# One program region from the neighbourhood attention to the soft experts, and one activation table for logarithm and exponential

## The chip, the cores and the metric

The kernel runs on one core of a Trainium2 chip, in float32 with a few bfloat16 matrix products. The metric is the device time of one launch in microseconds. A core has five engines that each run their own instruction queue in order: TensorE (PE, matrix products; the weight loads are listed apart as PEld), VectorE (DVE), ScalarE (ACT), GpSimd (POOL) and SyncE (SP, which issues most DMAs). They meet only through semaphores: an instruction waits until a counter has a value, and another engine's instruction raises it.

## The reference

Input are 32 rows of 512 token ids; the width is D = 64. With LN for a layer norm without parameters:

```
h = token_features(x)
h = h + neighbourhood_attention(LN(h))     # 8 heads, 31 neighbours, dilation 2
h = h + mixture(LN(h))                     # 8 experts, top 2 by a router, exact gelu
h = h + decayed_attention(LN(h))           # (q k^T / 8) * 0.99^(i-j), i >= j, no softmax
h = h + soft_experts(LN(h))

soft_experts(x):  feat = mean(x, batch);  w = softmax(feat @ Wr + br)        # [512, 8]
  a = relu(bn1(x @ W1[e] + b1));  a = relu(bn2(a @ W2[e] + b2))
  out = sum over e of (a @ Wo[e] + bo) * w[:, e]
```

## The kernel before

Two batch rows share a tile, 64 channels of each on 128 partitions by 512 tokens, so there are NP = 16 such pairs. `s.h` holds the running sum and `s.z` the normalised input of a stage. Every stage is a software pipeline written out by hand: `unrolled(count, unroll, (lead, step), ...)` emits each engine's steps in one fixed order, and `wait_ge` and `then_inc` tie the engines together. `done(n)` is n + 17, because the engine that frees a buffer first gives 16 credits (`give_credits`); a consumer that comes before the credits waits for them.

An `nc.Block()` is one program region. At its end all five engines meet at a barrier. Before the change there are six of them: preparation, token features, neighbourhood attention with the mixture of experts (these two already share one), `decayed_attention`, `soft_router` and `soft_experts`. The text calls the three joins between the last four stages seam A (mixture to decayed attention), seam B (decayed attention to soft router) and seam C (soft router to soft experts).

The layer norm has a side chain: POOL squares the pair (`square`, L488), PE sums the squares over channels (`variance`, L495), ACT turns them into a reciprocal deviation by Ln and Exp, SP sends the result through DRAM and back to all partitions (`hop`, `spread`, tiles `n_bc`), and POOL multiplies (`scaled`, L535). Four pairs go together. The last four pairs of a stage are scaled without DRAM, by PE (`near`, L2086) and DVE (L2155). In the mixture Ln and Exp run on ACT between gelu calls, twice: `last_deviations` (L1600, L1602) and `deviations` for n = 1 (L1642, L1644).

`soft_router` is a chain with little to overlap: the last four normalised pairs, PE sums of all 16 (`sums_of`, L2090), copy, logits, softmax on DVE and ACT, turn (L2112), copy (L2134), spread to expert weights (L2118), copies into `f1_w` (L2137, L2171) and `f1_r` (L2173). Then `soft_experts` runs 64 steps of `first` (PE L2225), `relu` (ACT L2272), `second` (PE L2235), `weigh` (DVE L2292), `third` (PE L2247), and per pair a residual (DVE L2303, L2306). `first` and `relu` need no router weights; `second` and `weigh` do. `keep_warm` (L502) issues small products whose results nobody reads.

## Time and profile before

| | us |
|---|---|
| median of 3 runs | 862.85 (859.15 to 865.65) |
| the profiled execution, its device time | 860.88 |
| its span from the first to the last instruction | 859.2 |
| PE busy in the span | 797.3 (93%) |
| DVE, ACT, POOL busy | 582.8, 480.8, 301.9 |

The span is the time between the first and the last recorded instruction; 1.7 us of the execution lie around it. Busy matrix products are pipelined records, so 93% does not say that PE works at its peak, only that it has little empty time. Idle time of an engine matters where the others wait for it.

### The profile page before, as it was taken

What the parts mean: (1) busy time and instruction counts of PE and PEld (TensorE: products, weight loads), DVE (VectorE), ACT (ScalarE), POOL (GpSimd) and SP (SyncE); (2) the same over time, 40 slices, a digit from 0 to 9 for tenths busy, and PEclk for the clock granted to TensorE, in tenths of its full rate; (3) what the DMA queues carried; (4) which work ended last, traced back from release to release, by engine and by line L of the source; (5) the groups of instructions that cost most, each with busy time, mean ns of one, the idle gap of its engine ahead of it and who ended that gap; (6) DMA issues with size and microseconds to landing.
All of it is one profiled execution on the core that took longest, in us unless ns stands there. A gap on an engine that the chain in (4) does not pass through costs nothing. (4 is left out here: it accounts for less than half of the span.)

```text
span 859.2 us, 28916 instructions
## 1 busy us (share of the span) xinstructions
PE 797.3 (93%) x12645; PEld 407.8 (47%) x12645; DVE 582.8 (68%) x853; ACT 480.8 (56%) x660; POOL 301.9 (35%) x292
## 2 busy tenths in 40 slices
PE   3989799999999999799899899899998899999996
PEld 2222377776676676523333233476663233333332
DVE  5537477777776776678687956577772477777776
ACT  2244477787777777666666766322222455555553
POOL 3225463543553442113453455465452900000000
PEclk9999899999999999999999999999999999999998
DMA  4210221001002001000200310153321011111111
GB/s 107 30 32 1 87 65 41 4 4 65 4 5 65 5 4 65 3 2 1 62 2 1 99 50 2 26 174 100 98 76 37 14 50 50 50 44 40 43 51 37
DMA packets 38670, 36.38 MB, mean 42 GB/s; under 512 B 20817, under 2 KB 25074, under 8 KB 38418
## 3 DMA queue, kind: packets, MB, share of 16 engines
q1 hardware_dynamic: 37474, 32.52, 13.5%
q8 instruction: 101, 1.65, 0.8%
q10 hardware_dynamic: 1072, 2.02, 0.7%
q14 instruction: 23, 0.19, 0.1%
HBM read 18.79 MB, written 7.34 MB: 30 GB/s over the span
## 5 line engine op out<-in xcount | busy, mean ns | idle before, releaser
L2272 ACT ACTIVATE se_a<-se_p,cols 128x512 f32<-128x512 f32 x128 | 92.8, 775 | 75.9 <-PE se_p L2225 75.9
L2292 DVE SCALAR_TENSOR_TENSOR se_a<-se_p,cols,z 128x1024 f32<-128x1024 f32 x64 | 82.2, 1284 | 48.9 <-PE se_p L2235 48.9
L1264 DVE TENSOR_REDUCE na_rowmax<-na_ps 128x16 f32<-128x1024 f32 x64 | 78.1, 1220 | 53.5 <-PE na_ps L1108 53.5
L1589 ACT ACTIVATE z<-me_p,cols 128x512 f32<-128x512 f32 x128 | 81.1, 685 | 53.9 <-PE me_p L1511 51.2
L1772 DVE TENSOR_TENSOR me_gw<-me_pc,z 128x1024 f32<-128x1024 f32 x64 | 78.3, 1223 | 45.1 <-PE me_pc L1528 36.8
L944 POOL TENSOR_TENSOR z<-na_k,const 128x512 f32<-128x512 f32 x62 | 63.0, 1047 | 127.8 <-ACT na_k L1186 127.8
L488 POOL TENSOR_TENSOR n_sq<-h 128x512 f32<-128x512 f32 x64 | 68.5, 1075 | 82.5 <-DVE h L858 39.8
L1546 PE MATMUL me_py<-me_gw,w_out 64*64 64x512 f32 x512 | 90.9, 607 | 0.0
L1511 PE MATMUL me_p<-z,moe_w 64*64 64x512 f32 x512 | 82.3, 611 | 2.0 <-ACT z L1589 2.0
L535 POOL TENSOR_TENSOR z<-h,n_bc 128x512 f32<-128x512 f32 x58 | 74.4, 1297 | 23.8 <-DMA n_bc<-n_spread 23.8
L1267 DVE TENSOR_TENSOR z<-na_ps,na_rowmax 128x1024 f32<-128x1024 f32 x64 | 78.4, 1225 | 2.2
L1117 PE MATMUL na_pt<-const,z 128*128 128x128 f32 x512 | 70.1, 280 | 5.3 <-ACT z L1213 3.1
L1213 ACT ACTIVATE z<-z 128x1024 f32<-128x1024 f32 x64 | 67.4, 1053 | 7.1 <-DVE z L1267 6.4
L2225 PE MATMUL se_p<-z,f_w 64*64 64x512 f32 x512 | 68.7, 603 | 2.0 <-ACTq L548 1.1
L2235 PE MATMUL se_p<-se_a,f_w 64*64 64x512 f32 x512 | 68.2, 598 | 1.3 <-DVE se_a L2292 1.3
L1220 ACT ACTIVATE na_et<-na_pt 128x1024 f32<-128x1024 f32 x64 | 65.4, 1021 | 6.7 <-PE na_pt L1117 5.9
L2247 PE MATMUL se_py<-se_a,w_out 64*64 64x512 f32 x512 | 67.4, 589 | 0.5 <-DVE se_a L2292 0.5
L1117 PEld LDWEIGHTS na_pt<-const,z 128*128 128x128 f32 x512 | 56.8, 142 | 21.0 <-issue 15.1
L1108 PE MATMUL na_ps<-z,na_q 32*32 32x256 f32 x2048 | 51.2, 386 | 0.6 <-issue 0.5
L1131 PEld LDWEIGHTS na_po<-na_v,na_et 128*32 128x32 f32 x4096 | 41.6, 110 | 21.1 <-ACT na_et L1220 11.4
L1207 ACT ACTIVATE na_v<-na_pm 64x512 f32<-64x512 f32 x64 | 38.6, 603 | 21.4 <-PE na_pm L1063 21.0
L1131 PE MATMUL na_po<-na_v,na_et 128*32 128x18 f32 x4096 | 48.0, 187 | 1.6 <-issue 0.9
(363 smaller groups left out, 1260.9 us busy)
## 6 DMA issues: line engine op xcount, KB each, us to landing
n_bc<-n_spread SPq DMA_DIRECT2D x116, 128.0 KB, 3.1
z<-z SPq DMA_DIRECT2D x64, 128.0 KB, 2.4
out<-se_rows SPq DMA_DIRECT2D x16, 256.0 KB, 2.1
n_spread<-n_rstd SPq DMA_DIRECT2D x12, 256.0 KB, 2.0
const<-in_const ACTq DMA_DIRECT2D x1, 1114.0 KB, 7.4
const<-in_const ACTq DMA_DIRECT2D x1, 562.0 KB, 4.5
f_w<-in_L_ffn_W SPq DMA_DIRECT2D x4, 128.0 KB
const<-in_const ACTq DMA_DIRECT2D x1, 258.0 KB, 2.9
```

Of the source, the lines that this page charges most:

```text
L535: return eng.tensor_tensor(row(s.z, p), row(s.h, p), s.bc[p % 4][:], ALU.mult)
L1117: mm = nc.tensor.transpose(p_t[:, c, :], e[b][:, 2 * c:2 * c + 2, :].rearrange("p h w -> p (h w)"), const(s, "ident"))
L1131: mm = nc.tensor.matmul(p_o[QT * t:QT * t + QT, at_col:at_col + 18], et[b][:, head, QT * t:QT * t + QT], v[j % 2][:, par * 4 + t, b, head, ...
L1264: nc.vector.tensor_reduce(rowmax[b][:], scored, AX, ALU.max).then_inc(s_max, 1)
L1267: nc.vector.tensor_tensor(e[b], scored, rowmax[b][:].unsqueeze(2).broadcast_to([128, GROUPS, WIN]), ALU.subtract).then_inc(s_diff, 1)
L1511: mm = nc.tensor.matmul(hidden(at.n, b)[half[e2], :], s.moe_w1[half[b], 2 * ep + e2, :], row(s.z, at.of(4))[half[b], :], start=True, stop= ...
L1546: mm = nc.tensor.matmul(p_y[half[b], e2, :], s.moe_w2[half[e2], ep, :], gw[at.k % 2][half[e2], b, :], start=(ep == 0 and b != e2), stop=(e ...
L1589: nc.scalar.activation(g[at.n % 7][:, b, :], hidden(at.n, b)[:], ACT.Gelu, bias=col(s, "moe_b1", ep)).then_inc(s_g, 1)
L1772: nc.vector.tensor_tensor(gw[at.k % 2][:], p_c[:], g[at.n % 7], ALU.mult).then_inc(s_gw, 1)
L2225: mm = nc.tensor.matmul(hidden(at.n, e2)[half[b], :], s.f1_w1[half[e2], 2 * ep + e2, :], z[half[e2], :], start=True, stop=True, skip_group ...
L2272: nc.scalar.activation(a1[at.k % 2][:, e2, :], hidden(at.n, e2)[:], ACT.Relu, scale=col(s, "f1_g1", 2 * ep + e2), bias=col(s, "f1_be1", 2 ...
L2292: nc.vector.scalar_tensor_tensor(out=a2[at.k % 2][:], in0=p_2[:], scalar=col(s, "f1_be2", ep), in1=s.f1_w[:, ep, :].unsqueeze(1).broadcast ...
```

## The change

The last three blocks are gone: `decayed_attention`, `soft_router` and `soft_experts` put their instructions behind those of the mixture in the same region, and their semaphores live as long as it does. Where the barriers kept order, single waits do now: POOL clears the attention's state once the mixture's last sum is done (`s_end`), PE's first `scores` wait for the mixture's sums to leave their PSUM banks, SP waits for `s_qk`, and `second` and `weigh` wait for the router's copies (`s_taken`, `s_kept`).

Work is moved over the seams too. The last `variance`, Ln and Exp of the attention are issued in the router's code, PE having eight `sums_of`, the scale product and the shift product ahead of them. Pairs 9 to 11 are scaled by DVE in place of POOL. The four `near` products signal one by one. `first(0)` and `first(1)` stand around the expansion of the weights on PE, `relu(0)` between the router's copies on ACT. POOL's 16 additions of `f1_r` are paced by `first`. Five groups of `keep_warm` go or shrink: 7 to 0, 8 to 0, 8 to 3, 4 to 2, 8 to 0; one of 2 is new.

The mixture loads the table set with both logarithm and exponential ahead of each Ln, where a set was loaded for Ln and another for Exp. The attention loads it behind its second `fetch`, the router not at all.

```diff
-                if at.n == EP * NP - 1:
-                    keep_warm(nc, s, p_r[:], 7)
...
+                    sc.preload_act_table_set("natural_log_exp_and_others")
...
+                        nc.vector.tensor_tensor(row(s.h, i), row(s.h, i), odd[slot][:], ALU.add).then_inc(s_end, 1)
...
-        block = ctx.enter_context(nc.Block())
...
+            pool.wait_ge(s_end, 1)
...
-                if p >= 6:
+                if 6 <= p < NP - 1:
...
-            normal(NP - 6)
-            normal(NP - 5)
...
+                if at.n == 0:
+                    te.wait_ge(s_even, done(NP - 1))
+                    te.wait_ge(s_odd, done(NP - 1))
...
-            spreads(NP // 4 - 1, NP - 1)
-            keep_warm(nc, s, p_s[:, 0, :], 8)
...
-            sc.preload_act_table_set("natural_log_exp_and_others")
             give_credits(sc, s_qkd)
 
             def former(at):
                 if at.n > 0:
                     return
+                sc.preload_act_table_set("natural_log_exp_and_others")
...
-            deviations(NP // 4 - 1)
...
-        p_sums, p_scale, p_small, p_shift, *p_wide = [ps(x) for x in ("psums", "pscale", "psmall", "pshift", "pwide0", "pwide1", "pwide2", "pwide3")]
...
+        *p_near, p_sums, p_small, p_shift, p_scale, p_last = [ps(x) for x in ("pnear0", "pnear1", "pnear2", "psums", "psmall", "pshift", "pscale", "plast")]
+        p_near.append(p_last)
+        p_wide = [p_small, p_shift, p_scale, p_last]
...
+                sp.wait_ge(s_qk, done(NP - 2 + p))
...
-            for j in range(4):
-                mm = nc.tensor.matmul(p_wide[j][:], const(s, "near")[group(j), :], s.rstd[group(j), LAST, :], start=True, stop=True, skip_group_check=True)
-            mm.then_inc(s_near, 1)
...
-            for p in range(ENDS[0]):
+            for p in range(8):
...
-            te.wait_ge(s_z, 4)
+            te.wait_ge(s.n_z, nth(3, 8))
+            sums_of(8)
+            te.wait_ge(s.n_sq, nth(3, NP - 1))
+            variance(nc, s, LAST, p_small).then_inc(s.n_var, 1)
+            te.wait_ge(s.n_z, nth(3, 11))
+            for p in range(9, 12):
+                sums_of(p)
+            keep_warm(nc, s, p_near[0][:], 2)
+            te.wait_ge(s.n_rstd, quad(3, LAST))
+            for j in range(4):
+                nc.tensor.matmul(p_near[j][:], const(s, "near")[group(j), :], s.rstd[group(j), LAST, :], start=True, stop=True,
+                                 skip_group_check=True).then_inc(s_near, 1)
             for p in ENDS:
+                te.wait_ge(s_z, p - ENDS[0] + 1)
                 mm = sums_of(p)
             mm.then_inc(s_sums, 1)
             keep_warm(nc, s, p_small[:], 3)
...
-            keep_warm(nc, s, p_shift[:], 8)
+            keep_warm(nc, s, p_near[2][:], 3)
+
+        def expand_weights(te):
             te.wait_ge(s_copies, 1)
...
-            keep_warm(nc, s, p_small[:], 4)
+            keep_warm(nc, s, p_small[:], 2)
...
-            keep_warm(nc, s, p_small[:], 8)
+            nc.tensor.matmul(p_sums[:], shift[:], by_expert[0:32, :], start=True, stop=True, skip_group_check=True).then_inc(s_shifted, 1)
...
-            sc.preload_act_table_set("natural_log_exp_and_others")
...
+            sc.wait_ge(s.n_var, quad(3, LAST))
+            nc.scalar.activation(s.rstd[:, LAST, :], p_small[:], ACT.Ln, bias=s.eps[:]).then_inc(s.n_ln, 1)
+            sc.wait_ge(s.n_ln, 8 + LAST)
+            nc.scalar.activation(s.rstd[:, LAST, :], s.rstd[:, LAST, :], ACT.Exp, scale=-0.5).then_inc(s.n_rstd, 1)
...
+
+        def fetch_turned_weights(sc):
             sc.wait_ge(s_turned, 1)
...
+        def fetch_weights(sc):
             sc.wait_ge(s_wide, 1)
             for ep in (0, 2):
-                nc.scalar.activation(s.f1_w[:, ep, :], p_wide[ep][:], ACT.Copy)
+                nc.scalar.activation(s.f1_w[:, ep, :], p_wide[ep][:], ACT.Copy).then_inc(s_taken, 1)
...
-            ve.wait_ge(s_near, 1)
-            for p in ENDS:
-                v.tensor_tensor(row(s.z, p), p_wide[p % 4][:], row(s.h, p), ALU.mult).then_inc(s_z, 1)
+            ve.wait_ge(s.n_z, nth(3, 8))
+            for p in range(9, 12):
+                ve.wait_ge(s.n_bc[p % 4], spread_done(3, p))
+                scaled(nc.vector, s, p).then_inc(s.n_z, 1)
             ve.wait_ge(s_scale, 1)
             w2 = s.f1_w2[:].rearrange("p a b -> p (a b)")
             v.scalar_tensor_tensor(out=w2, in0=p_scale[:], scalar=float(HID), in1=w2, op0=ALU.mult, op1=ALU.mult)
+            for p in ENDS:
+                ve.wait_ge(s_near, p - ENDS[0] + 1)
+                v.tensor_tensor(row(s.z, p), p_near[p % 4][:], row(s.h, p), ALU.mult).then_inc(s_z, 1)
...
-                v.tensor_copy(s.f1_w[:, ep, :], p_wide[ep][:])
...
-            v.tensor_copy(s.f1_r, p_shift[:])
...
+            v.tensor_copy(s.f1_r, p_sums[:]).then_inc(s_kept, 1)
...
+            pool.wait_ge(s_kept, 3)
             for p in range(NP):
+                if p >= 2:
+                    pool.wait_ge(s_w1, done(EP * (p - 1)))
...
+                if at.n == 0:
+                    te.wait_ge(s_taken, 2)
+                    te.wait_ge(s_kept, 3)
...
-            unrolled(EP * NP, 8, (3, first), (2, second), (1, third), (0, turn))
+            def next_first(at):
+                if at.n >= 2:
+                    first(at)
+
+            first(Step(0, 0, 8))
+            expand_weights(te)
+            first(Step(0, 1, 8))
+            unrolled(EP * NP, 8, (3, next_first), (2, second), (1, third), (0, turn))
...
-            unrolled(EP * NP, 8, (0, fetch_odd), (3, relu))
+            def next_relu(at):
+                if at.n >= 1:
+                    relu(at)
+
+            fetch_turned_weights(sc)
+            relu(Step(0, 0, 8))
+            fetch_weights(sc)
+            unrolled(EP * NP, 8, (0, fetch_odd), (3, next_relu))
...
+                if at.n == 0:
+                    ve.wait_ge(s_taken, 2)
+                    ve.wait_ge(s_kept, 2)
...
+            sums = mixture_of_experts(nc, s, r, inner, block)
+            s_qk = decayed_attention(nc, s, inner, block, *sums)
+            weights = soft_router(nc, s, inner, block, s_qk)
+            soft_experts(nc, s, out, inner, block, *weights)
```

ACT in the mixture, from the router's copy to the return to gelu. The names are tiles: `n_rstd` the deviations, `me_odd` half of the expert sum, `me_pr` a PSUM bank. Before:

```order
L1577 ACTIVATE me_logits_t<-me_pr 128x512 [waits me_rt,me_rl]
L1600 ACT_TABLE_LOAD
L1600 ACTIVATE n_rstd<-n_rstd,eps 128x512 [waits me_last]
L1602 ACT_TABLE_LOAD
L1602 ACTIVATE n_rstd<-n_rstd 128x512 [waits n_s_ln]
L1610 ACTIVATE me_odd<-me_py 128x512 [waits me_hz,me_w2]
L1589 ACT_TABLE_LOAD [waits me_gw]
```

And changed:

```order
L1576 ACTIVATE me_logits_t<-me_pr 128x512 [waits me_rt,me_rl]
L1599 ACT_TABLE_LOAD [waits me_last]
L1600 ACTIVATE n_rstd<-n_rstd,eps 128x512
L1602 ACTIVATE n_rstd<-n_rstd 128x512 [waits n_s_ln]
L1610 ACTIVATE me_odd<-me_py 128x512 [waits me_hz,me_w2]
L1588 ACT_TABLE_LOAD [waits me_gw]
```

One table load stands there in place of two; the same holds at L1642 to L1644.

PE at seam B, from the attention's last variance to the sums of pairs 12 to 15. Before:

```order
L495 MATMUL da_pw<-n_sq,const 32x512 [waits n_s_sq,da_st]
L495 MATMUL da_pw<-n_sq,const 32x512 x3
L502 MATMUL da_ps<-pick_b,ident_b 128x512 x8
L1802 UNCONDITIONAL_BRANCH
L2083 UNCONDITIONAL_BRANCH [waits barrier_Pool_Activation_PE_DVE_SP_release]
L2086 MATMUL sr_pwide<-n_rstd,const 128x512 x4
L2090 MATMUL sr_psums<-z,w_in 32x512 x12
L2094 MATMUL sr_pscale<-bn_diag,const 128x512
L2097 MATMUL sr_pshift<-f_wdup,const 32x128 x4
L2090 MATMUL sr_psums<-z,w_in 32x512 [waits sr_z]
```

And changed, starting right behind the attention's last output product:

```order
L2090 MATMUL sr_psums<-z,w_in 32x512 x8
L2094 MATMUL sr_pscale<-bn_diag,const 128x512
L2097 MATMUL sr_pshift<-f_wdup,const 32x128 x4
L2090 MATMUL sr_psums<-z,w_in 32x512 [waits n_s_z]
L495 MATMUL sr_psmall<-n_sq,const 32x512 [waits n_s_sq]
L495 MATMUL sr_psmall<-n_sq,const 32x512 x3
L2090 MATMUL sr_psums<-z,w_in 32x512 [waits n_s_z]
L2090 MATMUL sr_psums<-z,w_in 32x512 x2
L502 MATMUL sr_pnear<-pick_b,ident_b 128x512 x2
L2110 MATMUL sr_pnear<-n_rstd,const 128x512 [waits n_s_rstd]
L2110 MATMUL sr_pnear<-n_rstd,const 128x512 x2
L2110 MATMUL sr_plast<-n_rstd,const 128x512
```

The independent sums, the scale and the shift moved from behind the `near` products to ahead of the variance; the sums of pairs 12 to 15 (`[waits sr_z]`) now follow `near` directly.

PE at seam C, from the turn of the weights on. Before:

```order
L2118 MATMUL sr_pwide<-sr_by_expert,const 128x512 [waits sr_by_expert]
L2118 MATMUL sr_pwide<-sr_by_expert,const 128x512 x3
L2121 MATMUL sr_pshift<-sr_by_expert,sr_shift 128x512 [waits sr_shift]
L502 MATMUL sr_psmall<-pick_b,ident_b 128x512 x8
L2051 UNCONDITIONAL_BRANCH
L2213 UNCONDITIONAL_BRANCH [waits barrier_Pool_Activation_PE_DVE_SP_release]
L2225 MATMUL se_p<-z,f_w 64x512 [waits se_s_a1,n_s_swapped0]
L2225 MATMUL se_p<-z,f_w 64x512 x3
L2225 MATMUL se_p<-z,f_w 64x512 [waits se_s_a1]
```

And changed:

```order
L2253 MATMUL se_p<-z,f_w 64x512 [waits se_s_a1,n_s_swapped0]
L2253 MATMUL se_p<-z,f_w 64x512 x3
L2126 MATMUL sr_psums<-const,sr_copies 128x128 [waits sr_copies]
L2126 MATMUL sr_psums<-const,sr_copies 128x128 x3
L502 MATMUL sr_psmall<-pick_b,ident_b 128x512 x2
L2132 MATMUL sr_psmall<-sr_by_expert,const 128x512 [waits sr_by_expert]
L2132 MATMUL sr_pshift<-sr_by_expert,const 128x512
L2132 MATMUL sr_pscale<-sr_by_expert,const 128x512
L2132 MATMUL sr_plast<-sr_by_expert,const 128x512
L2135 MATMUL sr_psums<-sr_by_expert,sr_shift 128x512 [waits sr_shift]
L2253 MATMUL se_p<-z,f_w 64x512 [waits se_s_a1]
```

`first(0)` (L2225, now L2253) moved ahead of the turn and `first(1)` directly behind the shift product.

## Rows read from the trace of the kernel before

**Rows 1.** Windows: PE, PEld, DVE, ACT, POOL busy; PE clock, DMA share, GB/s.

```profile
416.00:418.00 2.00, 2.00 (x16) 0.67 (x12) 0.00 (x0) 0.00 (x0) 0.00 (x0) 0.51 0.35 118
...
720.00:740.00 20.00, 20.00 (x184) 7.38 (x180) 14.80 (x23) 11.00 (x16) 0.00 (x0) 1.00 0.15 42
```

**Rows 2.** Timeline at the first Ln and Exp of the mixture.

```profile
411.57 1.28 ACT L1602 ACT_TABLE_LOAD   x1
...
413.40 0.58 ACT L1610 ACTIVATE me_odd<-me_py 128x512 f32<-128x512 f32 x1
414.08 0.69 PE L1542 MATMUL me_py<-me_ct,w_out 64*64 64x512 f32 x2 [3.09 <-issue]
418.62 1.27 ACT L1589 ACTIVATE z<-me_p,cols 128x512 f32<-128x512 f32 x2 [3.34 <-PE me_p L1511]
```

**Rows 3.** Timeline at the second Ln and Exp of the mixture.

```profile
478.60 1.28 ACT L1644 ACT_TABLE_LOAD   x1
...
483.98 1.09 PE L1511 MATMUL me_p<-z,moe_w 64*64 64x512 f32 x8 [1.22 <-ACT z L1589]
```

**Rows 4.** Timeline where neighbourhood attention meets the mixture, without a barrier.

```profile
365.95 0.66 PE L1511 MATMUL me_p<-z,moe_w 64*64 64x512 f32 x4
```

**Rows 5.** Timeline at seam A.

```profile
543.18 0.60 ACT L1610 ACTIVATE me_odd<-me_py 128x512 f32<-128x512 f32 x1 [3.37 <-PE me_py L1546]
...
543.91 0.69 DVE L1784 TENSOR_TENSOR h<-h,me_odd 128x512 f32<-128x512 f32 x1
...
544.99 1.28 ACT L1971 ACT_TABLE_LOAD   x1 [1.21 <-PEq L2363]
...
546.42 1.09 PE L1909 MATMUL da_pqk<-z,w_in 64*64 64x512 f32 x8 [1.69 <-ACT L1971]
```

**Rows 6.** Timeline at seam B, to the copy of the sums.

```profile
644.13 0.94 PE L1947 MATMUL da_py<-da_qd,da_state 128*128 128x128 f32 x6 [0.24 <-DVE da_state L2036]
...
645.87 1.04 POOL L488 TENSOR_TENSOR n_sq<-h 128x512 f32<-128x512 f32 x1 [1.36 <-DVE h L2042]
...
647.06 1.94 PE L495 MATMUL da_pw<-n_sq,const 128*32 128x512 f32 x8 [1.99 <-POOL n_sq L488]
...
649.05 0.69 ACT L1994 ACTIVATE n_rstd<-da_pw,eps 128x512 f32<-128x512 f32 x1 [10.32 <-PE da_pw L495]
...
649.77 0.63 ACT L1996 ACTIVATE n_rstd<-n_rstd 128x512 f32<-128x512 f32 x1
...
651.67 1.14 PE L2086 MATMUL sr_pwide<-n_rstd,const 32*128 32x512 f32 x8 [0.30 <-PEq L1802]
...
652.74 2.78 PE L2090 MATMUL sr_psums<-z,w_in 128*32 128x512 f32 x24
652.87 2.48 DVE L2155 TENSOR_TENSOR z<-sr_pwide,h 128x512 f32<-128x512 f32 x4 [7.08 <-PE sr_pwide L2086]
...
656.51 0.95 PE L2097 MATMUL sr_pshift<-f_wdup,const 128*32 128x128 f32 x7
...
658.52 0.60 ACT L2130 ACTIVATE sr_sums<-sr_psums 128x512 f32<-128x512 f32 x1 [0.64 <-PE sr_psums L2090]
```

**Rows 7.** Timeline from the router's turned weights over seam C.

```profile
662.91 0.60 ACT L2134 ACTIVATE sr_by_expert<-sr_psums 128x512 f32<-128x512 f32 x1 [1.74 <-PE sr_psums L2112]
...
664.87 1.08 ACT L2137 ACTIVATE z<-sr_pwide 128x512 f32<-128x512 f32 x2 [1.37 <-PE sr_pwide L2118]
...
666.08 0.68 DVE L2173 COPY z<-sr_pshift 128x512 f32<-128x512 f32 x1
...
668.55 1.09 PE L2225 MATMUL se_p<-z,f_w 64*64 64x512 f32 x8 [1.08 <-ACTq L548]
669.70 1.45 ACT L2272 ACTIVATE se_a<-se_p,cols 128x512 f32<-128x512 f32 x2 [3.75 <-PE se_p L2225]
...
674.24 1.28 DVE L2292 SCALAR_TENSOR_TENSOR se_a<-se_p,cols,z 128x1024 f32<-128x1024 f32 x1 [7.48 <-PE se_p L2235]
```

**Rows 8.** Timeline of DVE at the first residual of the soft experts.

```profile
686.47 1.56 DVE L2306 TENSOR_TENSOR se_res<-se_res,se_odd 128x512 f32<-128x512 f32 x1
```

36 lines of the change are left out of this document (17 added, 19 removed).

## The prediction

> **What bounds the kernel now.** I read the windows of 20 us first, to see whether an engine sets the pace, and then the timeline at the places that the change touches, following at each the wait that ends last.
>
> In the soft experts PE is busy without a gap at full clock: 20.00 of 20 us, clock 1.00 [rows 1]. Nothing in the change makes those 64 steps shorter, so time can only come from the places where PE stands still. There are five.
>
> In the mixture ACT interrupts its gelu for Ln and Exp. At the first place PE sits idle for 3.09 us until 414.08 [rows 2]; what ends it is the copy `me_odd`, which ACT finishes at 413.98 behind two table loads. PE's granted clock then falls to the lower level of 1.2 GHz, 0.51 over 416 to 418 [rows 1], and the next gelu starts only at 418.62. At the second place PE waits 1.22 us for ACT [rows 3].
>
> At seam A the last copy of the mixture ends at 543.78, but the attention's first product starts at 546.42: it waits for ACT, whose table load from 544.99 to 546.27 stands ahead of the credits that PE needs [rows 5]. At seam B PE's last output product ends at 645.07, the squares come at 646.91, the variance takes 1.94 us instead of the 1.09 that eight such records take elsewhere (the clock has dropped in the gap), Ln and Exp end at 650.40, the barrier costs until 651.67, and then PE does twelve sums, scale and shift although the pairs that the chain waits for were ready at 655.35; the copy of the sums starts at 658.52 [rows 6, 7]. At seam C the last copy of the router ends at 666.76, and DVE's first `weigh` starts at 674.24, since `first`, `relu`, `first`, `second` fill the pipeline only then [rows 7].
>
> **Do joints without a barrier cost anything?** The kernel already has one, between neighbourhood attention and mixture: PE's first product there starts at 365.95 with no idle time in its row [rows 4]. I take zero for the branch that remains.
>
> **The tables.** At the first place one load of 1.28 us goes [rows 2]. ACT reaches `me_odd` 1.28 earlier, and that copy is what PE waits for: 1.3 us. Bounds: 0 if another wait is right behind it; and up to 1.3 + 2.3 if the shorter idle time (3.09 - 1.28 = 1.81) also keeps the clock up, as half of the 4.54 us from 414.08 to 418.62 is what the lower clock can cost at most. Idle times of 1.69 at seam A left the clock alone, judging by the 1.09 of the eight records behind it [rows 5], and 1.99 at seam B did not [rows 6]; 1.81 lies between, so I count only the 1.3. At the second place the load saved is also 1.28, the wait that it can shorten is 1.22 [rows 3]: 1.2, bounds 0 and 1.28. Sum 2.5.
>
> From the start of the load at 411.57 to the copy at 413.40 pass 1.83 us, and an Exp lies between them [rows 2]: there is room for the 1.28 of the load and for little else. The Trainium skill, page "ScalarE: Activation LUTs", section "What ACT_TABLE_LOAD costs", gives about 1283 ns for the load and 1380 ns of drain on top, 2.66 us for a switch. By that price the two places would give 2.8 us more on ACT. The rows agree on the 1283 and leave no room for the drain, so the sum goes by the rows.
>
> **Seam A.** The table load moves behind the second `fetch`, where ACT waits for the next variance anyway; nobody waits for it there, and if that cover were too short it would cost at most its 1.28. The credits for the first product now stand right behind `me_odd`, which ends at 543.78 [rows 5]. So the product starts at about 543.9 instead of 546.42: 2.5 us. The values on DVE wait for POOL's clearing of the state, which now waits for the sum that ends at 544.60 [rows 5]; with a short clearing that is about 545.2, and the value products, behind the 1.09 us of the first, are done at about 546.1. The added wait is hidden by 0.9 us; everything queued behind it on POOL is the last square, which nobody needs yet. PE's new wait ahead of the first scores is for sums that are out of PSUM by 543.91, when DVE goes on to the next [rows 5], long before the scores' own inputs. The removed seven `keep_warm` leave PE idle for 0.8 us, less than the 1.69 that did no harm. Bounds 1.3 (ACT's load still in the way) and 3.3 (start at the end of the mixture's last product). Take 2.5.
>
> **Seam B.** PE after 645.07 does, without a barrier: eight sums at 2.78/12 = 0.23, 1.85; the scale, 655.52 to 656.51, 1.0; the shift, 0.95; one more sum, 0.23. That is 649.1 [rows 6]. POOL's squares are ready at 646.91, so the variance, which waits for nothing else, starts 2.0 us later than before. At full clock it takes 1.09 and ends at 650.2, 1.2 later than before. Ln and Exp 0.69 and 0.63: 651.6. The first `near` signals alone, 1.14/4 = 0.3: 651.95. DVE's four products take 2.48: 654.4. PE has nothing else left, so the last sum ends at about 654.75 and the copy starts at 654.8 against 658.52: 3.7 us. On the way DVE does three scalings of 0.69 (an addition of the same shape, [rows 5]) from 645.8, which must be done when PE comes to their sums at 650.2: 2.1 us of work in 4.4 us. Their data come from eight DMAs that landed before POOL used them. If POOL's square is held up by them, it has 2.0 us of slack. Bounds: 2.0 (the clock drops again while PE idles between the four products, and the small products behind take twice their time) and 4.5 (sums hidden better than I count). Take 3.7.
>
> That slack matters, because DVE and POOL do get in each other's way here: the residual with both inputs in SBUF took 1.56 us while POOL was adding [rows 8], and an addition of the same shape took 0.69 with POOL free [rows 5]. The Trainium skill, page "SBUF — State Buffer", section "SBUF: two separate sides", calls the shared pair an exclusive lock that whoever starts first keeps for the whole instruction. It speaks against putting the scalings on DVE just when POOL squares; by it the square could start up to 0.69 later, which the 2.0 us absorb, so the sum is the same.
>
> **Seam C.** The chain from the copy of the sums (658.52) to the end of `by_expert` (662.91 + 0.60) keeps its 5.0 us, except that `first(0)` stands before the turn on PE. It waits for ACT's credits, which stand behind the router's Exp, and then takes 1.09; DVE's four softmax steps run meanwhile. Bounds 0 and 1.09; I take 0.3. In the old times plus 0.3: `relu(0)`, 1.45, ends at 665.3, ACT's two copies, 1.08, at 666.4, DVE's `f1_r` at 667.06 [rows 7]. `second(0)` starts there, takes 1.09, and `weigh(0)` starts at 668.25 instead of 674.24: 6.0 us. `first(1)` and `relu(1)` are done by 668.1 and are not late, and with PE busy the drop of the clock that the pipeline's start had before has no gap to come from. SP's new waits for `s_qk` end with the attention's last projections, before the seam, with nothing but the fetches for the experts queued behind them. The eight `keep_warm` that go here cost nothing, because `first(1)` stands in their place. Bounds: 4.5 and 7.
>
> POOL's additions are spread out and leave the first residual alone: at most 0.87 [rows 8, 5], a part of which PE hides. Take 0.2.
>
> **Sum.** 2.5 + 2.5 + 3.7 + 6.0 + 0.2 = 14.9 us. The profiled execution took 860.9 (1.7 us around its span), so it becomes 846.0. The median of the three runs is 862.85, 2.0 above the profiled one, with runs from 859.15 to 865.65; against it the forecast is **848.0 us**, 1.7% faster. About 1% (8.6 us) is what a measurement of this kernel can tell from no change.
>
> **Rivals.**
>
> *The clock falls once more, and part is given back* (chance 0.15). 28 `keep_warm` products go on balance, and in seam B PE does only 0.23 us of work for each 0.62 us of DVE. If the clock drops there, what PE does until the experts run (logits, turn, spread, `first`, `second`: about 5 us at full clock on the chain) takes up to twice as long. For: the 1.94 us of the variance [rows 6] show that such a gap is enough. Against: ahead of it PE now has 5 us of unbroken work. Price 3 to 5: 851 to 853.
>
> *The clock stays up in the mixture* (0.17). The idle time of 1.81 is short enough, and the timing at the second place improves likewise. 2 to 4 us more: 844 to 846.
>
> *It does not do what it says* (0.07). The seams are serial chains, and only the waits for the barrier go, about 1.2 us of them at each seam by ACT's idle 1.21 [rows 5]; with the tables 3.6 + 2.5 = 6: about 857. Against: rows 6 and 7 show the work that is overlapped, and the queues of the changed kernel show it moved.
>
> *Slower: POOL's additions collide in every pair* (0.03). Before, the 16 additions of about 1.27 us ran in one go and could meet one residual or two. Now one runs per pair, 16 in all, and a collision of DVE's two-input residual with one costs 0.87 [rows 8, 5], at most the 1.27 of the whole addition. DVE's delay reaches PE over the residual, its turn and the PSUM bank. It decides from 14.9/16 = 0.93 us per pair; at 1.27 the kernel would take 868. Against: the addition for pair p is released by `first` of the pair before, two pipeline steps (5 us) ahead of the residual.
>
> The forecast itself has 0.58, its own range being 845 to 851. The range for 8 in 10 takes in both clock cases and the runs' scatter of 3 us: 841 to 854.5. Faster by over 1% means below 854.2: forecast, both clock cases and scatter, 0.88. Within 1%: 0.09. Slower by over 1%: 0.03.
>
> **What would show it.** In the changed profile: one table load each ahead of L1600 and L1642, PE idle about 1.8 us there and perhaps no dip of the clock; the first product of the attention within 0.2 us of the end of `me_odd`; the attention's 16 steps unchanged; from the last output product to the copy of the sums 9.7 us in place of 13.5; from that copy to the first `weigh` 9.7 in place of 15.7; then 16 equal pairs. Wrong would be: a clock of 0.5 in the router, a late DMA ahead of DVE's scalings, PE waiting for `second(0)` on something other than `f1_r`, or residuals of 1.56 us in many pairs.

## The result, and the profile of the changed kernel

Twelve runs of the changed kernel have a median of 858.89 us (853.75 to 862.16), twelve of the kernel before beside them 861.92 (857.62 to 869.11). The ratio is 0.9951, with a 95% interval from 0.9928 to 0.9975: about 4 us faster, where 14.9 were forecast. The time lies outside the range of 841 to 854.5.

The profiled execution took 859.43 us, its span 857.6. It starts with a handicap: at the first `weigh` of the mixture, ahead of any changed code, it is 3.08 us later than the profile of before (the granted clock over 15 to 100 us is 0.92 there, 0.96 in before). So I read it by stages, as the distance between the same operation at each end. All profiles of this study are read in that way:

| stage (us) | before | after | difference | forecast |
|---|---|---|---|---|
| mixture, first to last `weigh` | 159.88 | 157.91 | -1.97 | -2.5 |
| last `weigh` to first attention output added (seam A) | 14.13 | 11.40 | -2.73 | -2.5 |
| attention, first to last output added | 90.38 | 93.07 | +2.69 | 0 |
| last output added to first `weigh` of the experts (B, C) | 29.14 | 21.41 | -7.73 | -9.7 |
| experts, first to last `weigh` | 175.38 | 180.20 | +4.82 | -0.2 |

The five differences sum to -4.92. The seams gave 10.46 of the 12.2 forecast for them; two stages gave back 7.51 that the forecast did not have.

**The mixture's first place** (timeline of the changed kernel; columns: start, us, engine, line, operation, idle time before it and who ended it):

```profile
412.61 1.28 ACT L1599 ACT_TABLE_LOAD   x1
413.91 0.72 ACT L1600 ACTIVATE n_rstd<-n_rstd,eps 128x512 f32<-128x512 f32 x1
414.66 0.63 ACT L1602 ACTIVATE n_rstd<-n_rstd 128x512 f32<-128x512 f32 x1
...
415.80 1.28 ACT L1588 ACT_TABLE_LOAD   x1
415.88 0.65 PE L1543 MATMUL me_py<-me_ct,w_out 64*64 64x512 f32 x2 [1.81 <-issue]
...
418.72 1.27 ACT L1588 ACTIVATE z<-me_p,cols 128x512 f32<-128x512 f32 x2 [1.64 <-PE me_p L1512]
```

One load ahead of Ln, Exp right behind it without a second. PE is idle for 1.81 us instead of 3.09 and the next gelu waits 1.64 instead of 3.34 [rows 2]. From the 14th to the 15th `weigh` pass 4.80 us instead of 7.78: 2.98 are gone, more than the 1.28 of the load, since the clock did not fall. Another 1.10 is lost two steps on, where a small DVE operation took 1.51 us instead of 0.42 beside a multiplication of POOL:

```profile
422.76 1.27 POOL L535 TENSOR_TENSOR z<-h,n_bc 128x512 f32<-128x512 f32 x1 [0.44 <-DMA n_bc<-n_spread]
422.81 1.51 DVE L1714 TENSOR_TENSOR me_best<-me_best,const 128x256 f32<-128x256 f32 x1
```

At the second place ACT is ready earlier (PE's wait for it 0.31 instead of 1.22 [rows 3]), but DVE is the next limit, held by POOL in the same way (a cast that takes 0.28 us elsewhere takes 1.35 here, and 1.36 in the profile of before); behind the loss of 1.10, the rest of the mixture gave 0.08 in all.

```profile
483.89 1.09 PE L1512 MATMUL me_p<-z,moe_w 64*64 64x512 f32 x8 [0.31 <-ACT z L1588]
...
488.68 2.72 POOL L535 TENSOR_TENSOR z<-h,n_bc 128x512 f32<-128x512 f32 x2
...
488.93 1.35 DVE L1757 CAST me_ctin<-me_high 128x256 f32<-128x256 bf16 x1
```

**Seam A.** The copy `me_odd` (L1610, from 544.29, 0.60) ends at 544.89, and by then the attention's first product runs:

```profile
544.29 0.60 ACT L1610 ACTIVATE me_odd<-me_py 128x512 f32<-128x512 f32 x1 [3.37 <-PE me_py L1547]
...
544.46 1.09 PE L1910 MATMUL da_pqk<-z,w_in 64*64 64x512 f32 x8 [0.23 <-ACTq L548]
```

The 1.69 us of idle time in the profile of before [rows 5] are 0.23.

**Seam B.** The output products end at 646.14 (L1951, 645.20 and 0.94), the copy of the sums starts at 658.02: 11.9 us where 13.5 stood and 9.7 were forecast.

```profile
646.94 1.42 POOL L488 TENSOR_TENSOR n_sq<-h 128x512 f32<-128x512 f32 x1 [1.61 <-DVE h L2043]
...
651.84 0.69 ACT L2142 ACTIVATE n_rstd<-sr_psmall,eps 128x512 f32<-128x512 f32 x1 [1.50 <-PE sr_psmall L495]
652.56 0.63 ACT L2144 ACTIVATE n_rstd<-n_rstd 128x512 f32<-128x512 f32 x1
...
653.24 0.70 PE L2110 MATMUL sr_pnear<-n_rstd,const 32*128 32x512 f32 x3 [0.91 <-ACT n_rstd L2144]
...
654.40 1.89 DVE L2182 TENSOR_TENSOR z<-sr_pnear,h 128x512 f32<-128x512 f32 x3 [4.29 <-PE sr_plast L2110]
655.14 2.84 PE L2090 MATMUL sr_psums<-z,w_in 128*32 128x512 f32 x8 [0.76 <-DVE z L2182]
656.20 0.68 DVE L2182 TENSOR_TENSOR z<-sr_plast,h 128x512 f32<-128x512 f32 x1
...
658.02 0.60 ACT L2146 ACTIVATE sr_sums<-sr_psums 128x512 f32<-128x512 f32 x1 [4.83 <-PE sr_psums L2090]
```

The exponential ends at 653.19 where its forecast, moved by the 1.07 us between the profiles at this point, was 652.7. The first of the four products on `pnear` lets DVE start after 1.16 us, not 0.3: they stand on four groups of 32 rows, run side by side (note the second record of each beginning at 653.77) and finish together. And the copy starts 1.14 us after the end of the last `z` (656.88), where I had counted 0.4. The square on POOL and the three scalings on DVE did hold each other up, as the prediction feared: 1.42 us instead of 1.04 [rows 6] for the square, 2.73 instead of 2.1 for the scalings. PE came to the variance only 1.5 us behind the square's end (648.36), so this cost nothing.

**Seam C.** From that copy at 658.02 to `weigh(0)` at 667.58 pass 9.56 us, against 15.72 before [rows 7] and 9.7 by the forecast:

```profile
662.40 0.60 ACT L2152 ACTIVATE sr_by_expert<-sr_psums 128x512 f32<-128x512 f32 x1 [1.74 <-PE sr_psums L2126]
662.89 1.44 ACT L2310 ACTIVATE se_a<-se_p,cols 128x512 f32<-128x512 f32 x2
...
667.58 1.28 DVE L2340 SCALAR_TENSOR_TENSOR se_a<-se_p,cols,z 128x1024 f32<-128x1024 f32 x1 [1.44 <-PE se_p L2266]
```

**The experts.** The pairs are equal, as forecast, but 11.55 us long instead of 11.16, from the second to the fourteenth. One pair, from the timeline:

```profile
696.71 0.69 DVE L2379 TENSOR_TENSOR se_rows<-se_pt,se_along 128x512 f32<-128x512 f32 x1
...
697.21 1.27 POOL L2239 TENSOR_TENSOR h<-h,z 128x512 f32<-128x512 f32 x1 [10.28 <-PE se_p L2253]
697.43 1.08 DVE L2382 COPY se_rows<-se_first 128x8 f32<-128x8 f32 x1
...
698.42 1.27 DVE L2340 SCALAR_TENSOR_TENSOR se_a<-se_p,cols,z 128x1024 f32<-128x1024 f32 x1
698.63 1.05 PE L2253 MATMUL se_p<-z,f_w 64*64 64x512 f32 x8
699.84 1.09 PE L2266 MATMUL se_p<-se_a,f_w 64*64 64x512 f32 x8 [0.16 <-DVE se_a L2340]
```

The residual (L2354) takes 0.69 us in all 16 pairs. What is held is the tiny copy of the tile `se_first` into `se_rows`. It starts while POOL adds and ends when POOL ends, and the `weigh` behind it comes so late that PE waits: its product on `se_a` starts 1.21 us after the group before it, where 0.86 is the distance elsewhere in the pair. That is the 0.4. The group's row (columns: shortest, median, longest in ns):

```profile
L2382 DVE COPY se_rows<-se_first x16: 174/1078/1087, 685.9 to 854.8; 128x8 f32<-128x8 f32 x16
```

**The attention.** Step 11 takes 8.96 us instead of 6.59. PE waits there 1.74 us for the projections' data (0.93 before), and the windows of 2 us (busy time of PE, its weight loads, DVE, ACT, POOL; granted clock; DMA share; GB/s) show the clock fall to its lower level. So the 2.37 us have two parts: the wait is 0.81 longer, and the rest comes with the fallen clock.

```profile
618.05 1.09 PE L1910 MATMUL da_pqk<-z,w_in 64*64 64x512 f32 x8 [1.74 <-DMA z<-z]
```

```profile
616.00:618.00 2.00, 0.31 (x12) 0.17 (x6) 1.90 (x6) 0.00 (x0) 1.23 (x2) 1.00 0.66 206
618.00:620.00 2.00, 1.95 (x20) 1.14 (x22) 0.40 (x2) 0.80 (x2) 0.61 (x1) 0.88 0.78 212
620.00:622.00 2.00, 2.00 (x20) 1.78 (x20) 1.20 (x2) 0.47 (x1) 0.86 (x1) 0.50 0.73 216
622.00:624.00 2.00, 2.00 (x20) 1.55 (x18) 0.43 (x2) 0.00 (x0) 0.00 (x0) 0.77 0.42 98
```

SP's queue shows where the lateness begins. L507 writes the reciprocal deviations out (256 KB) and L519 reads them back; between the two issues stands the landing of the first:

```profile
610.57 0.33 SPq L507 DMA_DIRECT2D n_spread<-n_rstd  x1
613.58 1.10 SPq L519 DMA_DIRECT2D n_bc<-n_spread  x2
```

3.01 us, against 2.01 before. The view of the DMA, cut to 610 to 614.5 (rate in slices of 0.11 us), has a possible cause to offer:

```profile
GB/s 0 0 0 0 0 0 0 0 146 0 0 0 146 382 382 328 382 382 182 18 18 0 18 18 18 18 36 0 0 0 0 0 0 0 0 0 0 0 0 0
...
q8 instruction: 1, 0.02, 1.6%
```

The first 146 is a block of 16 KB that queue 8 fetches, PE's instructions. The transfer behind it runs at some 380 GB/s and is nearly done after 0.8 us, but then a tail of 18 GB/s goes on for 0.9 us, as if one of the 16 engines had begun late. That tail's cause inside the DMA is not shown. In the profile of before that block was fetched at 609.5, 2.4 us ahead of the transfer.

### The profile page after: what moved, and what is told of

Its sections match the earlier page's. It is cut to its first block, busy times and chain, and to the rows that moved or that the text cites. A ratio compares the mean times of both kernels' runs of the same rounds, so it can differ in the third digit from the quotient of the medians.

```text
span 857.6 us, 28821 instructions
## 1 busy us (share of the span) xinstructions
PE 796.0 (93%) x12611; PEld 407.7 (48%) x12617; DVE 595.6 (69%) x856; ACT 476.0 (56%) x657; POOL 299.2 (35%) x289
## 3 DMA queue, kind: packets, MB, share of 16 engines
q1 hardware_dynamic: 37474, 32.52, 13.5%
q8 instruction: 100, 1.64, 0.8%
q10 hardware_dynamic: 1072, 2.02, 0.7%
## 4 chain that ended last, share of the span: by engine, by line
PE 61%; issue 8%; DVE 8%; ACT 7%; POOL 2%; DMA 2%; SPq 1%; DVEq 0%; ACTq 0%; POOLq 0%
PE na_pt L1117 6%; PE se_p L2266 6%; PE me_p L1512 5%; PE se_p L2253 4%; PE me_py L1547 4%; PE na_ps L1108 4%; PE se_py L2278 4%; PE na_po L1131 3%; PE na_pm L1063 3%; DVE se_a L2340 2%; PE na_pm L1022 2%; ACT na_et L1220 2%; PE na_pm L1034 2%; ACT z L1213 2%; PE na_pm L1085 2%
## 5 line engine op out<-in xcount | busy, mean ns | idle before, releaser
L1547 PE MATMUL me_py<-me_gw,w_out 64*64 64x512 f32 x512 | 88.9, 601 | 0.0
L535 POOL TENSOR_TENSOR z<-h,n_bc 128x512 f32<-128x512 f32 x55 | 71.1, 1307 | 23.8 <-DMA n_bc<-n_spread 23.8
L2239 POOL TENSOR_TENSOR h<-h,z 128x512 f32<-128x512 f32 x16 | 20.4, 1276 | 156.3 <-PE se_p L2253 138.9
L2253 PE MATMUL se_p<-z,f_w 64*64 64x512 f32 x512 | 68.0, 596 | 0.2 <-ACTq L548 0.2
L1108 PE MATMUL na_ps<-z,na_q 32*32 32x256 f32 x2048 | 51.6, 390 | 0.2 <-issue 0.2
```

Of the source, the lines that this page charges most:

```text
L1108: mm = nc.tensor.matmul(p_s[b][QT * c:QT * c + QT, f, :, half, :], q[j % 2][r, par, t * QT:t * QT + QT], kblk[j % 2][r, :, par, w:w + WIN] ...
L1547: mm = nc.tensor.matmul(p_y[half[b], e2, :], s.moe_w2[half[e2], ep, :], gw[at.k % 2][half[e2], b, :], start=(ep == 0 and b != e2), stop=(e ...
L2253: mm = nc.tensor.matmul(hidden(at.n, e2)[half[b], :], s.f1_w1[half[e2], 2 * ep + e2, :], z[half[e2], :], start=True, stop=True, skip_group ...
```

## The experiments

Each edit is against the changed kernel unless it says otherwise. Each ratio is to runs of the kernel before that were made beside that row's runs, so rows are best compared by their ratios; 0.9951 is the ratio to hold them against.

| kernel | median us | ratio to before, 95% |
|---|---|---|
| changed kernel | 858.89 | 0.9951 (0.9928 to 0.9975) |
| e1, additions not paced | 859.83 | 0.9957 (0.9929 to 0.9985) |
| e2, paced one step later | 852.79 | 0.9873 (0.9840 to 0.9907) |
| e3, before + tables | 860.10 | 0.9968 (0.9943 to 0.9993) |
| e4, without the tables | 858.11 | 0.9956 (0.9927 to 0.9985) |
| e5, before + pacing | 865.76 | 1.0048 (1.0023 to 1.0073) |
| e6, + 64 idle waits of PE | 856.95 | 0.9943 (0.9919 to 0.9967) |
| e8, e2 + variance first | 851.14 | 0.9887 (0.9844 to 0.9930) |
| e9, e8 + 64 idle waits | 848.65 | 0.9862 (0.9824 to 0.9899) |
| e10, before + 192 idle waits | 876.05 | 1.0148 (1.0105 to 1.0192) |
| e11, e8 + 128 idle waits | 855.79 | 0.9925 (0.9899 to 0.9951) |
| e12, e9 without the tables | 850.78 | 0.9863 (0.9827 to 0.9898) |
| e13, e9 again | 850.41 | 0.9860 (0.9827 to 0.9893) |

### Where POOL's additions stand: e1, e2, e5

```diff
 # e1: both lines go;  e2: the second is changed;  e5: both are put into the kernel before
                 if p >= 2:
-                    pool.wait_ge(s_w1, done(EP * (p - 1)))
+                    pool.wait_ge(s_w1, done(EP * (p - 1) + 1))
```

> The changed kernel without the pacing wait ahead of GpSimd's additions to the residual in the experts (they run in one go, as in the kernel before). Theory A, the additions, now released by an expert step's signal, hold VectorE's small copy of the weighted rows' tile (1.08 us instead of 0.17) in nearly every pair, and this is the 0.40 us by which each pair is longer (11.56 instead of 11.16): the pairs are back at 11.16 us, first to last weigh of the experts 4 to 5 us shorter than in the changed kernel, total about 854.5 us where the changed kernel has 859. Rival B, the pairs are longer for another reason (the weights of the experts arrive later against an earlier start, or the order in one region): pairs stay at 11.56 us and the total stays within 1 us of the changed kernel.

> The changed kernel with the pacing wait put one expert step later (the addition is released by the weigh after the one that releases it now), so that GpSimd's addition of 1.3 us lies beside VectorE's weighing and not beside its small copy. Theory A (collision at one place of the pair): pairs at 11.16 us, 4 to 5 us less than the changed kernel, the same as without the wait within 1 us. Rival B (not the collision, but the weights or the order): no change. Rival C (any addition inside a pair costs, wherever it lies, since GpSimd and VectorE exclude each other on SBUF): pairs stay 0.3 to 0.5 us long with another instruction of VectorE as the one held.

> The kernel before, with nothing of the change but the pacing wait ahead of GpSimd's additions. The profile of before has one residual of VectorE held by the run of additions (1.56 us instead of 0.69), the one of the early tables 3.28 us, the changed kernel without the wait 6.68 us. Theory A: the wait takes that away (at most 0.9 us here) and puts the small copy's 0.9 us into every pair instead, pairs of 11.55 instead of 11.16 us: first to last weigh of the experts 180.2 instead of 175.4 us, 4 to 5 us slower than before. Rival B (the long pairs need the one region): pairs of 11.16 us, same time as before within 1 us.

Without the wait (e1) the pairs are 11.16 us again, all but one: the second takes 17.97. The experts take 181.93 us, more than the 180.20 with the wait. Both theories had missed this. Timeline of e1:

```profile
676.65 11.10 POOL L2237 TENSOR_TENSOR h<-h,z 128x512 f32<-128x512 f32 x9
681.62 6.68 DVE L2352 TENSOR_TENSOR se_res<-se_res,se_odd 128x512 f32<-128x512 f32 x1
...
688.36 0.92 PE L2287 MATMUL se_pt<-const,se_res 128*128 128x128 f32 x3 [5.28 <-DVE se_res L2352]
```

DVE's residual needs two operands from SBUF, as POOL's additions do. While POOL works through its queue without a gap it does not get in between two additions; it ends 0.55 us after the whole run does (687.75). The 1.56 us on which the prediction rested [rows 8] was the luck of a run whose end was near: POOL was busy until 687.48 there, and the residual ended at 688.03, again 0.55 later; with the tables alone (e3) the same residual took 3.28, and the pair 14.77, and in e10, again the kernel before, it took 3.29 and ended 0.55 behind POOL's run. The luck has a source in that one profile: its clock fell while the experts' pipeline filled (0.51 over 672 to 674 us), which made the first `weigh` 1.7 us later than in e3, e5 and e10, and so let POOL come nearer to its end. Unpaced additions thus cost 0.2 to 6.8 us in one pair, by where the run ends; in the one region, where `weigh` starts earlier, they cost the most.

One step later (e2) all pairs are 11.15 to 11.16 us and the experts take 175.10, which is 5.10 less than in the changed kernel. By the times it is 0.9873 against 0.9951, 6.7 us. The addition now lies beside a `weigh`, which reads PSUM and SBUF and isn't held, and the copy has its old length:

```profile
684.05 1.29 POOL L2239 TENSOR_TENSOR h<-h,z 128x512 f32<-128x512 f32 x1 [9.89 <-PE se_p L2253]
684.87 1.28 DVE L2340 SCALAR_TENSOR_TENSOR se_a<-se_p,cols,z 128x1024 f32<-128x1024 f32 x1 [1.29 <-PE se_p L2266]
686.07 0.68 DVE L2351 TENSOR_TENSOR se_res<-se_py,h 128x512 f32<-128x512 f32 x1
686.78 0.69 DVE L2354 TENSOR_TENSOR se_res<-se_res,se_odd 128x512 f32<-128x512 f32 x1
...
L2382 DVE COPY se_rows<-se_first x16: 175/176/176, 681.7 to 845.2; 128x8 f32<-128x8 f32 x16
```

e5 gives the converse: the kernel before with nothing but the wait has pairs of 11.54 to 11.55 us, experts of 180.15 us, and is slower, 1.0048 (1.0023 to 1.0073). Neither the one region nor the earlier start is needed for the long pairs.

### The late transfer in the attention: e6, e10, e11

```diff
             nc.tensor.matmul(p_m[2][:, 0:1], house, col(s, "tok_b2"), ...).then_inc(s_x, 1)
             at = CONST_AT["place"][0] + 28
+            for _ in range(64):
+                te.wait_ge(s_x, 1)
```

> The changed kernel with 64 waits more on TensorE at the start of the kernel, on a semaphore that has long reached its value and at a place where TensorE waits 3.0 us for VectorE anyway. They do nothing but move TensorE's later instructions back in its program, and with them the moments at which a block of its instructions is fetched. Theory A: in each of the four profiles with one region a fetch of 16 KB of instructions falls within 0.2 to 1.1 us of the 256 KB transfer of the reciprocal deviations in the decayed attention, which then lands in 2.9 to 3.8 us instead of 2.0, and step 11 is 7.5 to 9.7 us long instead of 6.3 to 6.6; the 64 instructions bring the fetch some 2.5 us forward, the transfer takes 2.0 us again, step 11 is at most 6.7 us, the attention 90.4 to 91 us, and the total 1.5 to 3 us below the changed kernel's 858.9. Rival B: the fetch is not the cause (the late transfer comes from the order of the queue in the one region): the transfer takes 2.9 us or more wherever the fetch falls, total as the changed kernel within 1 us.

> The kernel before, with 192 idle waits of TensorE at its start and nothing else. 64 such waits brought the fetch of TensorE's instructions forward by some 3 us; in the profile of before the fetches stand 2.4 us ahead of and 9.9 us behind the issue of the 256 KB transfer at 612 us, so 192 waits should bring the later of the two onto it, within 1.5 us. Theory A (the fetch makes the transfer late): the transfer takes 2.9 to 3.8 us, step 11 of the attention 7.5 to 9.7 instead of 6.6 us, in the old kernel with its barriers; the whole attention 1 to 3 us longer, total 1 to 3 us above before (other transfers may gain or lose beside it). Rival B (the late transfer belongs to the one region, and the 64 waits cured it by chance): 2.0 us and 6.6 us as before.

> Pacing one step later, variance first, and 128 idle waits instead of 64. With 64 the fetch had left the transfer of the attention and met the fourth of the neighbourhood attention (3.3 and 3.9 us in two profiles, 2.2 to 2.4 without). With 128 it should stand about 3 us further ahead of each. Theory A: attention's transfer 2.0 us and its step 11 6.6 us as with 64 waits, total within 1.5 us of the version with 64. Rival: the next block's fetch comes onto one of them and it is 1 to 3 us slower.

In the profiles of the changed kernel, e1, e2, e4 and e8 the fetch stands 0.4 to 1.2 us behind the issue of the transfer ahead of step 11; the transfer takes 3.01, 3.71, 2.89, 3.76 and 3.41 us, and step 11 8.96, 9.71, 7.50, 9.72 and 9.46 us. Only e2 kept its clock there (1.00 over 614 to 622 us): its wait of 1.84 us is longer than the changed kernel's 1.74, and yet the step is 1.5 us shorter. Less PE's wait, the step is 5.66 us in e2 and in before, and 7.2 to 7.3 in the four whose clock fell. So the late transfer costs 0.8 to 1.6 us by itself, and the fallen clock about 1.6 more. In before, e3 and e5 the fetch is 2.3 to 2.4 us ahead, the transfer takes 2.01 and the step 6.3 to 6.7. With the 64 waits (e6) the fetch is at 604.6 and the transfer, from 607.41 on, takes 2.02:

```profile
607.41 0.33 SPq L507 DMA_DIRECT2D n_spread<-n_rstd  x1
609.43 1.10 SPq L519 DMA_DIRECT2D n_bc<-n_spread  x2
```

Step 11 is 6.61 us and the attention 90.33, against 93.07. So the regression of the attention came from the phase of PE's instruction fetches, in good part by way of the clock. What the time shows of it is small, 0.9943 against 0.9951, and other stages have a part in that: the waits themselves lengthen PE's idle time at the start from 3.00 to 3.50 us, and the same shift brought a fetch (334.2) onto such a transfer issued at 333.51 in the neighbourhood attention, which took 3.33 us instead of the 2.2 to 2.45 of the unshifted profiles, and that stage took 255.34 us where eight unshifted profiles have 251.57 to 253.64. One transfer of that stage, issued at 264 to 270 us, is hit in all the unshifted profiles, that of before included (266.80, 3.07 us, a fetch 0.42 us behind its issue). e9 has one late transfer there too and takes 252.64, e11 has one and takes 254.10; e6, e10, e12 and e13 have two and take 254.5 to 255.9.

The ratio of e10 is no measure of the fetches: its first `weigh` of the mixture comes 15.2 us later than in before, and the 192 waits alone make PE's idle time at the start 10.39 us instead of 3.00. Its attention is 93.74 us against 90.38. e10 missed the transfer that I had aimed at (625.69, 2.01 us) but hit three others behind the mixture, and two in the neighbourhood attention. The one at 600.33 took 3.19 us with a fetch at 600.8, and step 7 behind it 7.72 us instead of 6.89, with the clock at 1.00 (ten profiles with a transfer of 2.0 us there and a clock that stays have 6.83 to 7.58):

```profile
600.33 0.33 SPq L507 DMA_DIRECT2D n_spread<-n_rstd  x1
603.52 1.11 SPq L519 DMA_DIRECT2D n_bc<-n_spread  x2
...
608.00 1.09 PE L1911 MATMUL da_pqk<-z,w_in 64*64 64x512 f32 x8 [2.06 <-DMA z<-z]
```

The others took 2.52 and 3.57 us, with fetches within 0.9 us of the issue. Its step 11 is 9.11 us all the same: there a fetch at 630.2 met the L519 transfers issued at 630.12, the queue's next issue of another line came 2.27 us later, PE waited 1.84 us, and the clock fell (0.52 over 636 to 638 us). In e5 step 7 took 9.01 us and in e8 9.14, and there it is the clock that makes the difference: PE's waits of 1.79 and 1.86 us are no longer than the 1.92 of e3, whose clock stayed and whose step 7 is 7.58. Over all 14 profiles 112 transfers of L507 were issued with no second one beside them: the 26 with a fetch 0.27 to 1.51 us behind their issue took 2.89 to 3.99 us, the 86 others 2.00 to 2.45. So it isn't one transfer that is sensitive, but whichever the fetch meets. With 128 waits (e11) the rival's case came: the next block met the transfer at 588.97, which took 3.93 us, step 7 took 8.34, and the kernel is 5 to 7 us slower than e9. Of that, 0.7 to 1.0 us is the attention; some 2 us stand ahead of the neighbourhood attention's first row maximum (104.08 against 102.2). The waits are there more than the idle time covers: it is 3.00 us without them, 3.50 with 64, 6.95 with 128 and 10.39 with 192. The rest is scatter of the early stages or not explained.

### The order in the router: e8, e9, e13

```diff
 # e8, PE; on ACT the copy of the shift goes behind the exponential
+            te.wait_ge(s.n_sq, nth(3, NP - 1))
+            variance(nc, s, LAST, p_small).then_inc(s.n_var, 1)
             nc.tensor.matmul(p_scale[:], ...).then_inc(s_scale, 1)
-            ... the shift's products, sums_of(8)
-            te.wait_ge(s.n_sq, nth(3, NP - 1))
-            variance(nc, s, LAST, p_small).then_inc(s.n_var, 1)
-            ... sums_of(9) to sums_of(11)
             keep_warm(nc, s, p_near[0][:], 2)
             te.wait_ge(s.n_rstd, quad(3, LAST))
             ... the four products on p_near
+            ... the shift's products, sums_of(8) to sums_of(11)
```

> The kernel with the pacing one step later, and in the soft router the variance of the last tile moved ahead of the scale's and the shift's products, these and the sums of 8 to 11 behind or beside ScalarE's logarithm and exponential, ScalarE's copy of the shift behind its exponential. Theory A (the seam is bound by the chain square, variance, logarithm, exponential, products, sums, and the other products of TensorE stand in its way): the exponential ends some 2 us earlier after the last attention output, last output to first weigh of the experts 19.3 to 19.9 us instead of 21.4, total 1.5 to 2 us below the kernel with the pacing alone. Rival B (VectorE's three scaled tiles or the sums of the last tiles are the next limit): 0.7 us or less.

> Pacing one step later, the variance first in the router, and the 64 idle waits of TensorE together. If the three add up (Theory A of each): 4.8 and 2 and 1 to 2.5 us below the changed kernel, near 850 us. If the shift of the instruction fetches only moves the collision to another transfer (rival): no better than the version without the 64 waits.

> The version with pacing one step later, variance first and 64 idle waits once more, as the measure for the three beside it: 848 to 850 us, 13 to 15 us below before; by the profiles the experts 175.1 us, last attention output to first weigh 19.1 us, attention 90.3 to 90.8 us.

The exponential ends 2.29 us earlier after the last output (4.73 us instead of 7.02), and the first `weigh` comes after 19.12 us instead of 21.41: the gain goes through whole. Copy of the sums of e8, whose last output is added from 649.97 on, after 9.56 us where the changed kernel has 11.85:

```profile
659.53 0.60 ACT L2144 ACTIVATE sr_sums<-sr_psums 128x512 f32<-128x512 f32 x1 [2.34 <-PE sr_psums L2090]
```

By the times e8 can't be told from e2 (0.9887 against 0.9873, intervals of 0.004 each way): its attention in the profile took 95.50 us, with a fetch beside a transfer and a fallen clock at steps 7 and 11. With the 64 waits (e9) this is 90.70, and the median 848.65, ratio 0.9862; once more (e13) 850.41 and 0.9860. This is the fastest version of the study, 12 us below before and 7.7 us below the changed kernel by the ratios.

### The tables: e3, e4, e12

```diff
 # e3: these two lines alone, in the kernel before;  e4, e12: taken out
+                    sc.preload_act_table_set("natural_log_exp_and_others")
                     nc.scalar.activation(s.rstd[:, LAST, :], ..., ACT.Ln, bias=s.eps[:]).then_inc(s.n_ln, 1)
```

> The kernel before with the two early loads of the table that holds both logarithm and exponential in the mixture, and nothing else of the change. Theory A (the first place gains about 1.9 us, at the second ScalarE is ready earlier but VectorE is the next limit, 0 to 0.3 us): 1.5 to 2.5 us less than before. Rival B (the stage gains its 2.5 us and more, the changed kernel's profile fell on a bad second place): 2.5 to 3.5 us. Rival C (what ScalarE saves is waited for elsewhere): within 0.7 us.

> The changed kernel without the two early table loads in the mixture: one region and the pacing wait stay. Theory A (tables and region add up; region gives 2.7 at the first seam and 7.7 at the two others, the paced additions take 4.8, net -5.6 by the marks): 1.5 to 2.5 us more than the changed kernel, 3 to 6 us less than before by the marks, as far as the clock in the attention's steps does not take it back. Rival B (the region's gain is mostly taken back, by a clock that falls again in the decayed attention): within 1 us of the kernel before.

> The best version so far (pacing one step later, variance first, 64 idle waits) without the two early table loads in the mixture. By the marks of the profiles, the stretch from the 12th to the 44th weigh of the mixture took 84.5 us in the seven with the early tables and 86.6 in the three without. Theory A: 1.5 to 2.5 us slower than the same version with them, which runs beside it. Rival B (as the times of the changed kernel and of the region alone had it, 0.8 us apart the other way): within 0.7 us.

The three pairs of times don't agree on a size: -2.7 us in e3 (0.9968, with 1 outside its interval), but 0.9956 against 0.9951 of the changed kernel for e4, and 0.9863 against 0.9860 in e12. With intervals of 2 to 3 us each way, the last two can't tell 2 us from nothing. From first to last `weigh` the mixture took 157.14 to 159.55 us in nine profiles with the early tables, mean 158.01, and 157.68 to 160.68 in five without, mean 159.40: 1.4 us less, with a scatter as large between single executions.

A narrower stretch tells more. Up to the 12th `weigh` all 14 profiles agree within 0.02 us. From the 12th to the 31st, which takes in the first place alone, they have 50.6 to 51.6 us with the early tables and 52.7 to 53.3 without, 1.8 apart in the mean and without overlap. Between the 14th and the 15th stand 7.72 to 7.78 us in the five without, whose clock fell each time; 4.80 in eight with them, whose clock stayed; and 6.50 in e13, where PE's idle time is the same 1.81 us but the clock fell:

```profile
416.46 0.65 PE L1545 MATMUL me_py<-me_ct,w_out 64*64 64x512 f32 x2 [1.81 <-issue]
```

```profile
417.00:419.00 2.00, 2.00 (x16) 0.71 (x12) 0.00 (x0) 0.66 (x1) 0.00 (x0) 0.57 0.23 87
```

So the load is worth 1.28 us there and the clock 1.70; about 1 us of it is lost again in the steps behind. From the 31st to the 44th, over the second place, the means differ by 0.2. Theory A's 1.9 and 0 to 0.3 are what the profiles show in the stage itself; what is left of them at the end of the kernel, between 0 and 2.7 us, the times don't resolve.

## Why the prediction was wrong, step by step

**POOL's additions, "take 0.2".** The main failure, -0.2 forecast and +4.8 measured. The rival of the additions that collide in every pair had a chance of 0.03, and its mechanism is what happened, at 0.4 us a pair instead of the 0.93 that would have made the kernel slower; e2 and e5 show it from both sides. I had tested the wrong instruction. The residual stands two steps behind the addition, as written, but I didn't ask what else DVE does at the moment of release, and a copy of 128x8 elements didn't look like a victim. The Trainium skill, page "SBUF — State Buffer", section "SBUF: two separate sides", names as DVE's side of the lock operations with two inputs in SBUF and also those in a two-port mode; I had asked only for the two-input residual and not for the copy. The runs agree that one-input operations are held (the copy, 1.08 us instead of 0.17) and go further in one point: in before, e1, e3 and e10 DVE's residual didn't come in between two of POOL's instructions either, and ended 0.55 us behind the whole run.

**"The attention's 16 steps unchanged".** +2.7 us, in a stage whose code hardly changed. The step that failed is one that I didn't write: that removing instructions ahead of a stage leaves the stage as it was. The products, barriers and branches that went moved PE's later fetches by some 2.8 us against the transfers: one of them came to stand beside the transfer, PE waited 0.8 us longer for it, and the clock fell. e6 takes it back, e10 and e11 bring the late transfer about elsewhere.

**Seam B, 3.7.** 1.6 us measured between the two profiles, 0.9 to 1.8 against the three others of the kernel before in this stage. The mechanism was right and three terms were off: the variance ended later, interleaved with sums of 9 to 11; the first signal of the four products took 1.16 instead of 0.3; the way from the last `z` to the copy 1.14 instead of 0.4. Together that is 2.1 us. I had divided the length of a row of many products by their number, which is PE's rate, where the chain pays the full passage of one. e8 shows that the order bound the seam: the variance placed first gives 2.29 us, and the copy of the sums then starts 9.6 us after the output, where I had forecast 9.7.

**Seam C, 6.0.** 6.16 measured between the two profiles, 9.56 us against 9.7 forecast for the changed kernel. That the term came out is in part luck, though. The profile of before is the only one of its code whose clock fell at this seam (0.51 over 672 to 674 us), and its 15.72 us stand against 14.00 to 14.02 in the three others (e3, e5, e10): against those seam C gave 4.4 to 4.5 us, the lower bound, and 1.7 of the forecast's 6.0 were a fall of the clock that does not belong to every execution. From last output to first `weigh` the profile of before has 29.14 us, the three others 27.70, 27.66 and 26.69; against those both seams gave 5.3 to 6.3 us, not 7.7.

**Seam A, 2.5.** 2.73 measured, 11.40 or 11.41 us in every profile with one region and 14.13 in each without.

**The tables, 2.5.** 1.97 between the two profiles and 1.4 over fourteen. At the first place the rival of a clock that stays up came true in eight of nine profiles (2.98 us instead of 1.3 between two `weigh`, of which the clock is 1.70 where I had bounded it by 2.3; 1.8 are left at the 31st), and at the second nearly the lower bound of 0: ACT was not what ended the wait once it was earlier. The price of a table switch by the Trainium skill, page "ScalarE: Activation LUTs", section "What ACT_TABLE_LOAD costs", with its 1380 ns of drain, doesn't show here either: Ln starts 0.02 us behind the end of the load.

**The other clock rival,** a fall in the router, didn't occur: the windows from 642 to 686 us show 1.00.
